# Beginning a keep-choice attention inside the routed layer before it

## The reference

```python
x = x + ffn(_layernorm(x))          # layer 1
x = x + attn_b(_layernorm(x))       # layer 2

def ffn(x):                         # 16 experts, the best 2 of each token, and a shared one
    shared = silu(x @ Sg) * (x @ Su) @ Sd
    topk_p, topk_i = top_k(softmax(x @ Wr), 2)
    return shared + sum_over_experts(weight * (silu(x @ wg) * (x @ wu) @ wd))

def attn_b(x):                      # 16 heads of 8 features, 512 tokens
    q, k, v = split(x @ w_attn.T, 3)
    importance = softmax(causal(q @ k.T * 8 ** -0.5)).mean(over queries)
    importance[-64:] = 1.0
    idx = top_k(importance, 391)
    out = softmax(q @ k[idx].T * 8 ** -0.5) @ v[idx]
    return out @ w_proj.T

def quantize(W):                    # weights of layers 5 and 7
    gamma = mean(abs(W))
    return clip(round(W / (gamma + 1e-5)), -1, 1)
```

## Time and profile before

| quantity | us |
|---|---|
| median of 3 runs | 2588.84 (2588.57 to 2590.8) |
| profiled execution, its own time | 2584.69 |
| its span, first to last instruction | 2582.9 |

### The profile page before, as it was taken

One profiled execution on the slowest core, in us unless ns is written; L12 is line 12 of the kernel. 1 busy time (PEld: TensorE's weight loads), 2 busy tenths in 40 slices (PEclk: granted clock), 3 DMA queues, 4 the chain that ended last, 5 costly groups with the idle time before them and its releaser, 6 DMA issues. The chain is left out here.

```text
span 2582.9 us, 29952 instructions
## 1 busy us (share of the span) xinstructions
PE 2178.0 (84%) x9736; PEld 884.6 (34%) x9776; DVE 1706.5 (66%) x2470; ACT 1225.5 (47%) x2451; POOL 698.8 (27%) x661
## 2 busy tenths in 40 slices
PE   8999999947559989977977779988878988878877
PEld 2333334312212224344433234433324436533333
DVE  5666675558887745554483664579995446669995
ACT  4656663148737763221363234346655422246653
POOL 1111110042201110121101010059981013139982
PEclk9999999979879989987887889999999999999999
DMA  4000000032000002000000000022210000012220
GB/s 164 1 1 1 1 1 1 1 50 38 13 2 1 1 1 98 1 1 1 1 1 0 1 1 1 1 84 94 92 61 1 1 1 2 1 60 97 92 82 16
DMA packets 24280, 68.62 MB, mean 27 GB/s; under 512 B 2816, under 2 KB 9024, under 8 KB 23360
## 3 DMA queue, kind: packets, MB, share of 16 engines
q1 hardware_dynamic: 23264, 65.94, 8.2%
q10 hardware_dynamic: 864, 0.79, 0.3%
HBM read 58.78 MB, written 1.57 MB: 23 GB/s over the span
## 5 line engine op out<-in xcount | busy, mean ns | idle before, releaser
L3810 POOL TENSOR_TENSOR l_drive<-l_du,l_bsb 128x1024 f32<-128x1024 f32 x126 | 296.3, 2374 | 38.6 <-DVE l_du L3711 26.3
L3562 DVE TENSOR_TENSOR_SCAN l_state<-l_decay,l_drive 128x1024 f32<-128x1024 f32 x128 | 290.0, 2278 | 10.0 <-ACT l_decay L3503 9.3
L3392 PE MATMUL l_py<-l_state,w_const 128*128 128x512 f32 x512 | 254.0, 622 | 41.2 <-DVE l_state L3570 29.6
L241 POOL TENSOR_TENSOR l_nx_small<-l_nx_small,w_norm 128x4 f32<-128x4 f32 x50 | 53.3, 1066 | 869.9 <-DVE l_nx_small L234 869.9
L403 ACT ACTIVATE l_probs<-l_psp,l_stats 128x512 f32<-128x512 f32 x256 | 172.9, 682 | 147.3 <-DVE l_stats L413 147.3
L3503 ACT ACTIVATE l_decay<-l_delta,l_a 128x511 f32<-128x511 f32 x256 | 164.9, 680 | 119.5 <-DVE l_state L3562 119.3
L1324 DVE TENSOR_REDUCE l_tops<-l_ring 128x2 f32<-128x1024 f32 x128 | 151.5, 1220 | 45.5 <-PE l_ring L1315 45.1
L411 DVE TENSOR_REDUCE l_stats<-l_psp 128x2 f32<-128x1024 f32 x128 | 156.1, 1220 | 29.4 <-PE l_psp L363 28.9
L760 DVE SCALAR_TENSOR_TENSOR l_product<-l_psu,w_gated,l_first 128x512 f32<-128x512 f32 x104 | 78.0, 750 | 130.9 <-ACT l_first L734 130.6
L1396 ACT ACTIVATE l_shared<-l_ring 128x512 f32<-128x512 f32 x256 | 139.1, 598 | 46.1 <-PE l_ring L1386 45.8
L3392 PEld LDWEIGHTS l_py<-l_state,w_const 128*128 128x128 f32 x512 | 99.6, 198 | 150.9 <-issue 84.0
(11 more groups left out here) (626 smaller groups left out, 4170.8 us busy)
## 6 DMA issues: line engine op xcount, KB each, us to landing
l_bsb<-l_rows SPq DMA_DIRECT2D x64, 512.0 KB, 3.6
l_csb<-l_rows SPq DMA_DIRECT2D x32, 256.0 KB, 3.2
l_stack<-l_parts SPq DMA_DIRECT2D x84, 64.0 KB
w_gated<-in_gated SPq DMA_DIRECT2D x1, 3297.5 KB, 10.6
w_mha<-in_mha SPq DMA_DIRECT2D x1, 2568.5 KB, 11.9
w_ssm<-in_ssm SPq DMA_DIRECT2D x2, 1171.0 KB, 14.5
w_moe<-in_moe SPq DMA_DIRECT2D x1, 2248.0 KB, 19.2
w_const<-in_const SPq DMA_DIRECT2D x1, 1131.0 KB, 14.2
```

Source lines behind the costliest of these rows:

```text
L3392: mm = pe.matmul(py[:, t, :], eye, state[:, k % STATES, t, :], start=False, stop=k % NS == NS - 1, skip_group_check=True)
L3562: dve.tensor_tensor_scan(state[:, k % STATES, :, :].rearrange("p t s -> p (t s)"), decay[:, k % 2, :, :].rearrange("p t s -> p (t s)"), dr ...
L3810: pool.tensor_tensor(drive[:, k % RING, :, :], du[:, :, :], bsb[:, k // 2 % RING, k % 2, :].unsqueeze(1).to_broadcast([P, CT, S]), ALU.mult)\
```

## The change

A class `KeepFront` holds what the front of the keep-choice layer needs: its semaphores, one buffer of parts, the remainders, the stack of batch 0. `routed_ffn` of layer 1 gets it as `guest` and works for it. Weight sums come after tile 13, the total at 15, the scale at 17, the signs at 18 and 20. The two projections of batch 0 stand on TensorE at n = 36 (in the banks of tile 34), the high parts on ScalarE at 36, the remainders on VectorE at 36 and 37; the middle and low parts go to GpSimd, between its norm powers, and it fills both ones rows of batch 0 early. SP issues all query transfers of batch 0 in layer 1. ScalarE issues six of the keys at n = 38 and twelve at n = 44. The last six go out on SP at the head of layer 2.

Each transfer of 64 partitions is split in two: a first of 16 partitions (head pairs 0 and 1, semaphores `first0`, `first1`) and one of 48 (pairs 2 to 7, `loaded0`, `loaded1`). The column order of the weights (`in_part_rows`) is changed to match. Even and odd batches have semaphores and parts of their own; the odd parts lie in the memory of `v`, whose fill therefore moves behind the fold loop on GpSimd. Step 0 of a batch waits for the first set, the first step of the second head group (j = 1) for the rest. At the head of layer 2 the late norm is woven between the first steps; its bank is `acc` in place of `ring[5]`, and the wait for its result moves from `score1(2)` to the first `importance`.

```diff
+KT = KH // 2
+GROUPS = (range(0, 2), range(2, KT))
...
+class KeepFront:
+
+
+    SIGNALS = dict(ones_rows=2 * B, front=2 * B, high=2 * B, rest=2 * B, mid=2 * B, low=2 * B, first0=16 * 24 * 2,
+                   first1=16 * 24 * 2, loaded0=16 * 24 * 2, loaded1=16 * 24 * 2, rowsum=2, total=1, gamma=2, scaled=2, rounded=2, clipped=2)
+    SCALE = float(KHD) ** -0.5
+
+    def __init__(self, nc, core):
+        self.core, self.ctx = core, ExitStack()
+        self.signals = {key: Signal(nc.alloc_semaphore(f"keep_{key}"), per) for key, per in self.SIGNALS.items()}
+        self.parts, self.rest = self.sb(nc, "parts", [P, 2, 3, S], BF16), self.sb(nc, "rest", [P, 2, S])
+        self.stack = self.sb(nc, "stack", [P, 2, KT, S], BF16)
+        self.rowsum, self.gamma = self.sb(nc, "rowsum", [P, 2]), self.sb(nc, "gamma", [P, 2])
+        self.signs = [core.w("bitffn", "w1"), core.w("bitffn", "w2")]
+        self.magic = 1.5 * 2.0 ** 23
...
+    def project(self, pe, i, bank):
+        pe.matmul(bank, self.core.w("keep", ("wq", "wk")[i]), self.core.xn[:, 0:S], start=True, stop=True)\
+            .then_inc(self["front"].sem, 1)
...
+    def high_part(self, act, i, bank):
+        act.wait_ge(self["front"].sem, self["front"].at(0, i + 1))
+        act.activation(self.parts[:, i, 0, :], bank, ACT.Copy, scale=(-self.SCALE, 1.0)[i]).then_inc(self["high"].sem, 1)
...
+    def rest_part(self, dve, i, bank):
+        dve.wait_ge(self["high"].sem, self["high"].at(0, i + 1))
+        dve.scalar_tensor_tensor(out=self.rest[:, i, :], in0=bank, scalar=(-self.SCALE, 1.0)[i],
+                                 in1=self.parts[:, i, 0, :], op0=ALU.mult, op1=ALU.subtract).then_inc(self["rest"].sem, 1)
...
+    def mid_part(self, pool, i):
+        pool.wait_ge(self["rest"].sem, self["rest"].at(0, i + 1))
+        pool.tensor_copy(self.parts[:, i, 1, :], self.rest[:, i, :]).then_inc(self["mid"].sem, 1)
+
+    def low_part(self, pool, i):
+        pool.wait_ge(self["mid"].sem, self["mid"].at(0, i + 1))
+        pool.tensor_tensor(self.parts[:, i, 2, :], self.rest[:, i, :], self.parts[:, i, 1, :], ALU.subtract)\
+            .then_inc(self["low"].sem, 1)
...
+    def load(self, queue, b, i, first, stack, parts, halves=(0, 1)):
+
+        n = 2 * b + i
+        queue.wait_ge(self["ones_rows"].sem, self["ones_rows"].at(0, n + 1))
+        queue.wait_ge(self["low"].sem, self["low"].at(0, n + 1))
+        pairs = GROUPS[0 if first else 1]
+        for h in halves:
+            at = h * HALF + pairs.start * KHD
+            for r, part in enumerate((Q_PARTS, K_PARTS)[i]):
+                to = h * HALF + r * KHD
+                queue.dma_start(stack[to:to + KHD, i, pairs.start:pairs.stop, :],
+                                parts[at:at + len(pairs) * KHD, i, "hml".index(part), :])\
+                    .then_inc(self[f"{'first' if first else 'loaded'}{b % 2}"].sem, 16)
...
+                    if guest and n == 15:
+                        guest.weight_total(pe, aux[:, 0:2])
+                    if guest and n == N:
+                        pe.wait_ge(L["product"].sem, L["product"].at(0, N - 1))
+                        pe.wait_ge(L["nx_xn"].sem, L["nx_xn"].at(0, 1))
+                        guest.project(pe, 0, psg[:, 0, :])
+                        guest.project(pe, 1, psu[:, 0, :])
                     if normed(n, 1) is not None:
+                        if guest and normed(n, 1) == 0:
+                            pe.wait_ge(guest["gamma"].sem, guest["gamma"].at(0, 1))
...
+                    if guest and n == N:
+                        guest.high_part(act, 0, psg[:, 0, :])
+                        guest.high_part(act, 1, psu[:, 0, :])
+                    if guest and n == N + 2:
+                        guest.load(act, 0, 1, True, guest.stack, guest.parts, (0,))
...
+                    if guest and n == N + 8:
+                        guest.load(act, 0, 1, True, guest.stack, guest.parts, (1,))
+                        guest.load(act, 0, 1, False, guest.stack, guest.parts, (0,))
...
+                    if guest and n == 13:
+                        guest.weight_sums(dve)
+                    if guest and n == 17:
+                        guest.weight_scale(dve, aux[:, 0:2])
+                    if guest and n in (18, 20):
+                        guest.weight_signs(dve, (n - 18) // 2)
+                    if guest and n in (N, N + 1):
+                        guest.rest_part(dve, n - N, (psg, psu)[n - N][:, 0, :])
...
+                if guest:
+                    guest.fill_ones(pool, 0)
+                    guest.fill_ones(pool, 1)
                 for b in range(inner):
                     nx.rstd(pool, b)
-
-            if load:
+                    if guest and b < 2:
+                        guest.mid_part(pool, b)
+                        guest.low_part(pool, b)
+
+            if load or guest:
                 @block.sync
                 def _(sync):
-                    load(sync)
+                    if load:
+                        load(sync)
+                    if guest:
+                        guest.load(sync, 0, 0, True, guest.stack, guest.parts)
+                        guest.load(sync, 0, 0, False, guest.stack, guest.parts)
...
+        rest = begun.rest
+        others = L.sb("stack", [P, B - 1, 2, KT, S], BF16)
+        stacks = [begun.stack] + [others[:, b, :, :, :] for b in range(B - 1)]
...
+        odd_parts = v[:, 0, :, :, :].rearrange("p t h c -> p (t h c)").bitcast(BF16)[:, 0:2 * 3 * S]
+        parts = (begun.parts, odd_parts.rearrange("p (i a s) -> p i a s", i=2, a=3))
...
-            if b:
-                act.wait_ge(L["loaded"].sem, L["loaded"].at(0, 16 * 24 * b))
-            act.activation(parts[:, i, 0, :], aux[:, :], ACT.Copy, scale=(-scale, 1.0)[i]).then_inc(L["high"].sem, 1)
+            if b >= 2:
+                act.wait_ge(L[f"first{b % 2}"].sem, L[f"first{b % 2}"].at(0, 16 * 24 * (b // 2)))
+                act.wait_ge(L[f"loaded{b % 2}"].sem, L[f"loaded{b % 2}"].at(0, 16 * 24 * (b // 2)))
+            act.activation(parts[b % 2][:, i, 0, :], aux[:, :], ACT.Copy, scale=(-scale, 1.0)[i]).then_inc(L["high"].sem, 1)
...
-            if j == 0 and s == 0:
-                pe.wait_ge(L["loaded"].sem, L["loaded"].at(0, 16 * 24 * (b + 1)))
+            if j < 2 and s == 0:
+                loaded = L[f"{'loaded' if j else 'first'}{b % 2}"]
+                pe.wait_ge(loaded.sem, loaded.at(0, 16 * 24 * (b // 2 + 1)))
             if x >= 3:
                 pe.wait_ge(L["exp1"].sem, L["exp1"].at(0, exps_through(x - 3)))
-            if x == 2 and last_in:
-                pe.wait_ge(L["in_xn"].sem, L["in_xn"].at(0, 1))
...
-            if c == 0:
-                pe.wait_ge(L["gamma"].sem, L["gamma"].at(0, 1))
+            if c == 0 and last_in:
+                pe.wait_ge(L["in_xn"].sem, L["in_xn"].at(0, 1))
...
-                project(pe, 0, 0)
                 if last_in:
                     late.centre(pe, B - 1)
-                project(pe, 0, 1)
-                weight_total(pe)
-                if last_in:
-                    late.var(pe, B - 1)
-                    late.spread(pe, B - 1)
                 pe.wait_ge(L["eye16"].sem, L["eye16"].at(0, 1))
                 pe.wait_ge(L["later16"].sem, L["later16"].at(0, 1))
-                pe.wait_ge(L["blank"].sem, L["blank"].at(0, 3))
                 score1(pe, 0)
+                if last_in:
+                    late.var(pe, B - 1)
                 score1(pe, 1)
+                if last_in:
+                    late.spread(pe, B - 1)
...
-                act.activation(stack[:, 0, 0, :, :].bitcast(F32), core.w("const", "q_ones").unsqueeze(2)
-                               .to_broadcast([P, KT, S // 2]), ACT.Copy).then_inc(L["ones_first"].sem, 1)
-                high_part(act, 0, 0)
-                if last_in:
-                    late.square(act, B - 1)
-                high_part(act, 0, 1)
                 act.activation(eye16[:, :], eye, ACT.Copy).then_inc(L["eye16"].sem, 1)
                 act.activation(later16[:, :], core.w("const", "later"), ACT.Copy, scale=-1.0)\
                     .then_inc(L["later16"].sem, 1)
-                load_stacks(act, 0, 1)
+                if last_in:
+                    late.square(act, B - 1)
...
-                weight_sums(dve)
-                for i in range(2):
-                    rest_part(dve, 0, i)
-                    mid_part(dve, 0, i)
-                    low_part(dve, 0, i)
-                    if last_in:
-                        (late.keep, late.eps)[i](dve, B - 1)
-                weight_signs(dve)
+                if last_in:
+                    late.keep(dve, B - 1)
+                maxima1(dve, 0)
+                if last_in:
+                    late.eps(dve, B - 1)
+                dve.memset(unit[:, :, :, :], 0.0).then_inc(L["blank"].sem, 1)
+                maxima1(dve, 1)
                 if last_in:
                     late.diag(dve, B - 1)
```

(34 more changed lines are left out.)

155 lines of the change are left out of this document (73 added, 82 removed).

## The result

| | kernel before | changed kernel |
|---|---|---|
| median, us | 2589.82 of 4 runs (2588.57 to 2592.52) | 2575.52 of 4 runs (2570.68 to 2577.72) |
| ratio, 95% interval | | 0.9947 [0.9932, 0.9962] |
| profiled execution, us | 2584.69 (span 2582.9) | 2577.72 (span 2575.9) |
| first score matmul, us | 545.80 | 521.50 |
| anchor (first sum over the folds), us | 558.51 | 542.24 |

Faster, as forecast, by 0.5%, but 14.3 us instead of 20.8, and 0.5 us outside the range. The profiled executions differ by 7.0 only, so I follow the time place by place.

The account below looks back on a forecast made before the run. It took the wait for one batch's preparation and transfers before layer 2's first score as the bound; 19.8 us at the anchor (layer 1's 3.0 cost included) plus 1.0 for the clock off 2588.84 gave 2568.0, range 2562 to 2575.

Parts of the forecast that it names:

- (E): Rival: first score waits as before, pieces starting only at layer 1's end; no gain, 2588 us; chance 0.03.
- (D): Rival: each transfer piece costs 0.93 us whatever its size, so later batches stall; slower, 2596 us; chance 0.05.
- (B): Rival: a fixed part per transfer makes the split delay batch 0's first set; 2571 to 2573 us; chance 0.16.
- terms (a) to (d): Layer 1's added weight sums, signs, projections and remainders: cost 3.0 us in sum, bounds 1.9 to 4.6.
- (a): Layer 1: two sums over weights on VectorE after tile 13 delay the next spreading matmul; cost 0.6 us.
- Term (e): Layer 1's transfer issues on SP and ScalarE: covered by VectorE's last work, SP done by 515, so no cost.
- The head: Layer 2's start to anchor: 20.1 us, held by GpSimd's copies, clearing and first fold; gain 19.8 us.
- Rival (A): GpSimd does not hold the head, as VectorE's stall is absorbed; gain 24.4 us, 2564.4 us; chance 0.18.
- unhindered 17.5: Layer 2's start to anchor if GpSimd's queue were not late: 17.5 us, a gain of 22.4 us.
- Later batches: Batches 1 to 3 in 48 pieces instead of 24: cost 0, with 1.5 us or more of cover.
- The clock behind the anchor: Choosing loop's first intervals: less time lost to TensorE's low clock, gain 1.0 us (0 to 2.3).
- a rate of 67 GB/s: Batch 0's transfers move at 67 GB/s: first set landed by about 514, 5 us before the first score.

Follow-up runs that it names:

- whole_all: Changed kernel with no transfer split, batch 0 included, all of batch 0 issued in layer 1; 2572.50 us, ratio 0.9936.
- best1: Changed kernel with early ones rows, whole transfers for batches 1 to 3, and batch 0's last six query pieces issued in layer 2; 2570.59 us.
- best_warm: best1 plus extra TensorE matmuls at layer 1's end, before the head's late spread and before later norm spreads; 2566.06 us, ratio 0.9916.
- pool_longer: Changed kernel with two more GpSimd copies of ones rows ahead of its first fold in layer 2; 2577.36 us, ratio 0.9959.
- again: Changed kernel run once more with no edit; 2571.71 us, ratio 0.9928 to the kernel before.
- again2: Changed kernel run a further time with no edit; 2571.50 us, ratio 0.9939 to the kernel before.
- before2: Kernel before run once more with no edit, for a second trace; 2589.01 us, ratio 1.0003.
- pool_early: Changed kernel with ones rows of batches 1 and 2 filled in layer 1, batch 3's between folds, clearing moved out of the head; 2570.74 us.

## Why the prediction was wrong

Right was the main mechanism: the 17.1 us wait for the stack went, the front fitted into layer 1, the anchor moved from 558.51 to 542.24, and no rival of another kind came true. Not (E): the first score waits for nothing. Not (D), nor (B): the first set had landed. The step that failed is the head of layer 2: I let GpSimd's queue decide there, at 20.1 us, and let VectorE's and TensorE's own work run at its undisturbed pace; VectorE's queue decided, at 22.2 to 23.0. Point by point:

- **Layer 1, terms (a) to (d).** Forecast 3.0; VectorE's last result is 3.0 later relative to the sums' start in all three traces. Its parts hold too: the spreading behind the weight sums moved from 432.39 to 433.00, the 0.6 of (a); the weighings stay 0.8 late through steady state (forecast 0.9 for the work on weights) and get 2.2 later with the projections and remainders (forecast 2.1).
- **Term (e), the issues.** Called covered. It failed by 0.7 us, and on SP, to which I gave 3 us of cover. I priced an issue at 0.61 to 0.67; they took 0.76 on the mean, from 499.81 on, and ended at 518.10 instead of 515. whole_all and best1, with fewer issues on SP, start layer 2 at 87.52 instead of 88.2.
- **The head.** Forecast 20.1 from the layer's start to the anchor, GpSimd last; measured 22.2 to 23.0, VectorE last. I had weighed the row on the slow diagonal, 1.54 us, and it came as forecast (1.42). What I missed is that it is not the only such operation. VectorE's middle part of batch 1 meets GpSimd's last copy and the clearing, its low part the fold, and they lose 2.0 and 0.5. The section of the Trainium skill that I cited (SBUF — State Buffer, "Who interferes with whom") covers both: besides instructions with two SBUF inputs, as the low part, it names casts in a two-port mode as contending, and says that whoever comes second is blocked for the whole instruction of the other. The trace agrees in kind, but the cast lost more than the rest of one instruction: in the three traces of this kernel it takes 2.42, 2.77 and 2.32 and ends 0.3 us behind the clearing each time, so it lost the rest of the last copy and the 0.95 of the clearing as well. I took from the section the one instruction that I already had a row for. The second part is the clock: fp32 pairs in the head at 2.07. I had granted that TensorE still idles there, and took only 1.0 of a possible 2.3 behind the anchor for it, but let the head's own matmuls stand at full clock; best_warm against best1 shows 1.7 us there.
- **Rival (A)**, that GpSimd doesn't hold, is half true: it doesn't hold directly (pool_longer: 1.7 to 2.0 of 3.8), but the gain of the rival, 24.4, asked for an undisturbed VectorE. With the copies gone the anchor is at 18.6, still 1.1 behind my unhindered 17.5, in which a slow diagonal of 1.0 was counted that is not there; with the clock kept up as well (best_warm) it is at 17.2.
- **Later batches.** Forecast cost 0 with 1.5 us of cover: a burst 10.5 us into the batch, 36 issues at 0.64 (23.0), landed at 36. The burst of 578.70 begins 11.2 us after the first step of batch 1 (567.51), 36 issues at the measured 0.71 take 25.6, and the first step of batch 2 stands 38.1 after that of batch 1, its last 1.0 a wait. So the issue rate, 0.71 against 0.64, is the mis-sized term. The later sets of batches 1 to 3 are waited for too, 0.2, 0.8 and 2.3. It was the term with the least room in my sum, and I gave it no price. What the waits cost is not shown: again has one of 2.2 and again2 one of 0.3, and both take longer from anchor to choice.
- **The clock behind the anchor.** Forecast 1.0 better; in the interval behind the anchor, which ends at 569.90 in the kernel before, it was 1.7 in all three traces, against the first trace of the kernel before, and 0.6 against before2. After that the traces of either kernel lose different amounts, up to 5 us, where the clock falls again.

The account: sums to anchor 110.85 on the mean, forecast 107.7, so 3.2 short. Anchor to choice, changed kernel 144.9 (mean of three) and kernel before 143.9 (mean of two): 1.0 lost where 1.0 was to be won, 2.0 short. Together 15.5 won instead of 20.8, close to the 16.2 of all runs. The 3.2 are shown: 0.7 the issues, the rest the head. The cause of the 2.0 stays open, and so does whether there is one, since two and three traces don't average a scatter of 5 us; the waits for transfers are not it by these traces. Nor is it shown whether the short waits for transfers bring on the falls of the clock: pool_early has 5.3 us of them and, from 543 up to 643 us, a full clock.

The range failed by its upper end, by 0.5 us. Part of that is chance: the medians of again and again2, for the same program, lie inside. The unknown costs were sized from one trace, and that trace lay 4 us under the median. I took the difference off the median rightly, but a range of 7 us above the forecast had little room for misses of the same sign.

One premise was wrong without a price: I took the transfers as a rate of 67 GB/s. The pieces of batch 0 moved at 82 to 90 GB/s once both queues issued, which leaves the first set more room, not less.

## What to carry to other kernels

When work moves beside other work, list every instruction of the neighbouring engine in that stretch, not the one that the profile happens to show slow. Splitting a transfer brings the anchor nearer where one batch waits for it (3.6 us here) and fills the issuing queue: compare the number of pieces times the time of one issue, as measured for such pieces, with the period. And trace the kernel before twice before a few us are forecast from it.
